# Macaron block on one core: the first step rebuilt, with four experts' weights spread by TensorE

## What is computed

```python
scores = sigmoid(x @ router_w.T); s = scores + bias        # 16 experts in 4 groups of 4
# best 2 groups by the sum of their two best s, then the best 4 experts in them
tw = scores[topk] / (sum + 1e-20) * 2.5                    # combine weights
h, u = einsum('td,edf->etf', x, gate_w), einsum('td,edf->etf', x, up_w)
y = einsum('etf,efd->etd', silu(h) * u, down_w)            # all 16 experts for all tokens
out = einsum('etd,te->td', y, combine) + shared_expert(x)  # shared: two more units of 128
```

## Time and profile before

| | us |
|---|---|
| median of 3 runs | 704.36 |
| profiled execution | 704.97 |
| its span on the core | 703.2 |
| TensorE busy | 667.4 (95%) |
| VectorE busy | 551.7 (78%) |
| GpSimd busy | 441.2 (63%) |
| ScalarE busy | 408.4 (58%) |

### The profile page before, as it was taken

How to read it: one execution, slowest core, us unless ns; L and a number is a source line. 1 busy time by engine, 2 the same in 40 slices (tenths; PEclk the granted TensorE clock), 3 DMA queues, 4 the chain that set the end, 5 groups by cost and what they waited for, 6 DMA issues and landing times.

```text
span 703.2 us, 11896 instructions
## 1 busy us (share of the span) xinstructions
PE 667.4 (95%) x3116; PEld 542.7 (77%) x3116; DVE 551.7 (78%) x1427; ACT 408.4 (58%) x812; POOL 441.2 (63%) x380
## 2 busy tenths in 40 slices
PE   4598999999999999999999999999999999999997
PEld 3386888888878878788776887768887888888885
DVE  4798887969697796977969869698697887969564
ACT  5465565565666545665456665566655565565553
POOL 4665666665766647665567565665657666666664
PEclk9699999999999999999999999999999999999999
DMA  8820633150605115042060320602406032240600
GB/s 230 264 93 4 239 121 121 33 209 2 240 1 195 47 31 212 0 152 89 6 236 0 123 118 17 240 0 100 156 15 240 11 147 100 70 188 17 240 15 16
DMA packets 30401, 76.31 MB, mean 109 GB/s; under 512 B 3584, under 2 KB 12304, under 8 KB 30352
## 3 DMA queue, kind: packets, MB, share of 16 engines
q1 hardware_dynamic: 30352, 75.79, 29.9%
HBM read 73.16 MB, written 2.62 MB: 108 GB/s over the span
## 4 chain that ended last, share of the span: by engine, by line
PE 64%; issue 12%; DVE 9%; POOL 9%; SPq 3%; DMA 1%; ACT 1%; DVEq 1%; POOLq 0%; ACTq 0%
POOL A_lo L319 8%; PE gateP L420 7%; PE gateP L422 7%; PE gateP L421 7%; PE upP L420 6%; PE upP L422 6%; PE upP L421 6%; PE yP L420 6%; PE yP L422 6%; PE yP L421 6%; DVE T L966 3%; SPq L255 1%; DVE A L988 1%; PE attP L466 1%; PE prepP L451 1%
## 5 line engine op out<-in xcount | busy, mean ns | idle before, releaser
L319 POOL TENSOR_TENSOR A_lo<-A,A_hi 128x512 fp32r<-128x512 f32 x288 | 370.9, 1292 | 193.5 <-ACT A_hi L708 193.3
L691 ACT ACTIVATE gateP<-gateP 128x512 f32<-128x512 f32 x256 | 148.7, 581 | 166.5 <-PE gateP L422 165.3
L966 DVE TENSOR_TENSOR T<-gateP,CB 128x512 f32<-128x512 f32 x256 | 175.1, 684 | 75.5 <-ACT gateP L691 67.8
L708 ACT CAST A_hi<-A 128x512 fp32r<-128x512 f32 x288 | 176.8, 614 | 74.9 <-DVE A L988 71.2
L988 DVE TENSOR_TENSOR A<-upP,T 128x512 f32<-128x512 f32 x256 | 176.9, 691 | 9.1
L420 PE MATMUL gateP<-XT_hi,W_hi 128*128 128x512 f32 x288 | 123.9, 430 | 13.9 <-DVE T L966 13.6
L420 PE MATMUL upP<-XT_hi,W_hi 128*128 128x512 f32 x288 | 114.7, 398 | 2.2 <-DVE A L988 2.2
L422 PE MATMUL gateP<-XT_lo,W_hi 128*128 128x512 f32 x288 | 113.8, 395 | 0.0
L420 PE MATMUL yP<-A_hi,W_hi 128*128 128x512 f32 x288 | 113.1, 393 | 0.6 <-POOL A_lo L319 0.6
L422 PE MATMUL upP<-XT_lo,W_hi 128*128 128x512 f32 x288 | 113.6, 395 | 0.0
L421 PE MATMUL gateP<-XT_hi,W_lo 128*128 128x512 f32 x288 | 113.5, 394 | 0.0
(11 more groups left out here) (162 smaller groups left out, 645.3 us busy)
## 6 DMA issues: line engine op xcount, KB each, us to landing
CB<-combT SPq DMA_DIRECT2D x128, 512.0 KB, 6.3
out_dram<-X SPq DMA_DIRECT2D x8, 256.0 KB, 2.0
X<-in_L_attn_x_dram SPq DMA_DIRECT2D x3, 512.0 KB, 6.0
W_in<-in_L_ffn_gate_w_dram SPq DMA_DIRECT2D x4, 256.0 KB, 4.8
W_in<-in_L_ffn_up_w_dram SPq DMA_DIRECT2D x4, 256.0 KB, 5.0
W_in<-in_L_ffn_down_w_dram SPq DMA_DIRECT2D x4, 256.0 KB, 5.2
X<-in_L_attn_x_dram SPq DMA_DIRECT2D x2, 256.0 KB, 4.3
combT<-CT SPq DMA_DIRECT2D x16, 32.0 KB, 1.8
```

The lines of the kernel that those rows point to most:

```text
L319: pool.tensor_tensor(A_lo[:, slot, :], A[:, slot, :], A_hi[:, slot, :].bitcast(F32), ALU.subtract).then_inc(low_done, 1)
L691: act.activation(dst, gateP[u % 2][:, :], ACT.Silu).then_inc(silu_done, 1)
L708: act.copy(A_hi[:, v % SLOTS, :], A[:, v % SLOTS, :]).then_inc(high_done, 1)
L966: dve.tensor_tensor(T[:, u % TS, :], gateP[u % 2][:, :], CB[:, e, :], ALU.mult).then_inc(gate_weighted, 1)
```

## The change

SP: the second half of X's first batch is loaded ahead of the shared weights instead of behind the first group of experts; of the other batches only batch 1 is loaded ahead of the first `CT` store, batches 2 and 3 and the small tensors behind the first step's `CB` loads. In step 0 the loads of experts 0 to 3 are left out.

TensorE: filler matmuls (`keep_busy`) at the start and ahead of the first `comb`; units 0 to 3 in an order of their own; experts 0 to 3 get their weights by `spread`, a transpose of a broadcast column of `comb`, into `backP` and `attP`; `transpose_weights(1)` moves from after unit 16 into unit 17; the setup transposes of the attention weights move from unit 6 to unit 20.

```diff
+    SPREAD = 4
+    WARM, FILL = 15, 10
 # SP
+            sp.dma_start(X[:, TILES:BT, :], x_v[0][:, TILES:BT, :]).then_inc(x_second, 16)
             ...
-                if g == 0:
-                    sp.dma_start(X[:, TILES:BT, :], ...).then_inc(x_second, 16)
-            for b in range(1, BATCH):
-                sp.dma_start(X[:, b * BT:(b + 1) * BT, :], x_v[b]).then_inc(x_rest, 16)
+            sp.dma_start(X[:, BT:2 * BT, :], x_v[1]).then_inc(x_third, 16)
             ...
-                for g in range(E // CSEM):
+                for g in range(SPREAD // CSEM if first else 0, E // CSEM):
             ...
             spread_weights(0, True)
+            for b in range(2, BATCH):
+                sp.dma_start(X[:, b * BT:(b + 1) * BT, :], x_v[b]).then_inc(x_rest, 16)
+            for dst, src in small:
+                sp.dma_start(dst, src).then_inc(small_in, 16)
 # GpSimd: constants first, then step_rstd(0), XA, and now
+            pool.wait_ge(xn_ready, 2)
+            step_rstd(1)
             ... # W_lo of units 2 and 3 in three pieces each, and in the pair
-                    if early and u < 3:
-                        split_low(2 * SHARED + 2 * u)
-                        split_low(2 * SHARED + 2 * u + 1)
-                    if early and w == 1:
-                        step_rstd(1)
+                    if early and u < AHEAD - 2 * SHARED:
+                        split_low(2 * SHARED + u)
 # TensorE
+            def spread(e):
+                for j in range(TILES):
+                    c = e * TILES + j
+                    mm = pe.transpose((backP, attP)[e % 2][:, j * P:(j + 1) * P],
+                                      comb[:, c:c + 1].broadcast_to([P, P]), ident[:, :])
+                mm.then_inc(spread_done, 1)
+            def keep_busy(count):
+                for _ in range(count):
+                    pe.matmul(yP[:, 0:P], ones[:, :], ones[:, :], start=True, stop=True)
+            def first_units():
+                for u in range(4):
+                    ... # waits: W_lo of u, XT_lo at u = 0, silu u - 2 from u = 2
+                    product(gateP[u % 2], ..gate..).then_inc(gate_done, 1)
+                    if u < 2:
+                        product(upP[u % 2], ..up..).then_inc(up_done, 1)
+                keep_busy(FILL)
+                pe.wait_ge(route_seq, ROUTE_OPS)
+                spread(0)
+                spread(1)
+                transpose_weights(0)
+                for u in (2, 3):
+                    pe.wait_ge(mul_done, u - 1)
+                    product(upP[u % 2], ..up..).then_inc(up_done, 1)
 # TensorE, pair: from unit 4
+                    if first and SHARED + 2 <= u < SHARED + SPREAD:
+                        pe.wait_ge(gate_weighted, u - SHARED - 1)
+                        spread(u - SHARED)
             ... # gate and up products of u
+                    if first and u == UNITS - 1:
+                        transpose_weights(1)
             ... # down product of u - 4
-                    if first and u == 6:
+                    if first and u == 20:
                         pe.wait_ge(small_in, 16 * 10)
-                        if w == (16 if early else 11):
+                        if w == 11 and not early:
                             transpose_weights(t0 + s + 1)
 # ahead of the pair
             pe.wait_ge(const_seq, IDENT_AT)
+            keep_busy(WARM)
 # ScalarE: W_hi of units 0, 1 ahead of XT; 2, 3 behind it; 4, 5 ahead of the pair;
 # 6 to 9 after silu 1; 10 and 11 in unit 3; 12 to 17 in units 4 to 9
+                        elif first and u < SHARED + SPREAD:
+                            if u >= SHARED + 2:
+                                act.wait_ge(mul_done, u - 1)
+                            dst = T[:, u % TS, :]
+                    if first and u in (3, 4):
+                        if u == 3:
+                            copy_weights(0)
+                        for v in (2 * u - 6, 2 * u - 5):
+                            round_high(n, v, False)
+                        if u == 3:
+                            split_high(AHEAD + 1)
 # VectorE
+                if isinstance(t, int) and t == 0 and e < SPREAD:
+                    dve.wait_ge(spread_done, e + 1)
+                    silu, weights = T[:, u % TS, :], (backP, attP)[e % 2][:, :]
             ...
-                    if early and w == 0:
-                        dve.wait_ge(x_second, 16)
-                        stats(1, 1)
-                    if first and u + AHEAD < UNITS:
-                        split_low(u + AHEAD)
+                    if first and 4 <= u and u - 4 + AHEAD < UNITS:
+                        split_low(u - 4 + AHEAD)
             ... # ahead of XT_lo
+            dve.wait_ge(x_second, 16)
+            rows(1, 1)
+            dve.wait_ge(rstd_ready, 2)
+            stats(1)
```

More of the change, by code:

```diff
@@ L236, in gate_left @@
         def gate_left(step, w):
-            if w < SHARED:
+            if w < SHARED or (isinstance(step, int) and step == 0 and w < SHARED + SPREAD):
                 return silu_done, UNITS * step + w + 1
@@ L311, in split_low @@
                 pool.wait_ge(w_hi_done, unit + 1)
-                pool.tensor_tensor(W_lo[:, unit, :, :], W_in[:, unit, :, :],
-                                   W_hi[:, unit, :, :].bitcast(F32),
-                                   ALU.subtract).then_inc(w_lo_done, 1)
+                if unit in (2, 3):
+                    for i in range(3):
+                        ins = pool.tensor_tensor(W_lo[:, unit, i, :], W_in[:, unit, i, :],
+                                                 W_hi[:, unit, i, :].bitcast(F32), ALU.subtract)
+                    ins.then_inc(w_lo_done, 1)
+                else:
+                    pool.tensor_tensor(W_lo[:, unit, :, :], W_in[:, unit, :, :],
+                                       W_hi[:, unit, :, :].bitcast(F32),
+                                       ALU.subtract).then_inc(w_lo_done, 1)
             def split_activations(n, slot):
@@ L520, in attention_stage @@
                         mm.then_inc(att_pe, 1)
+            def spread(e):
[9 more added lines that the diff above has]
+                for u in range(4):
+                    pe.wait_ge(w_lo_done, u + 1)
+                    if u == 0:
+                        pe.wait_ge(xt_lo_ready, 1)
+                    if u >= 2:
+                        pe.wait_ge(silu_done, u - 1)
+                    product(gateP[u % 2][:, :], W_hi[:, u, 0, :], W_lo[:, u, 0, :], XT_hi[:, 0, :],
+                            XT_lo[:, 0, :], True, True).then_inc(gate_done, 1)
+                    if u < 2:
+                        product(upP[u % 2][:, :], W_hi[:, u, 1, :], W_lo[:, u, 1, :], XT_hi[:, 0, :],
+                                XT_lo[:, 0, :], True, True).then_inc(up_done, 1)
+                keep_busy(FILL)
[5 more added lines that the diff above has]
+                    pe.wait_ge(mul_done, u - 1)
+                    product(upP[u % 2][:, :], W_hi[:, u, 1, :], W_lo[:, u, 1, :], XT_hi[:, 0, :],
+                            XT_lo[:, 0, :], True, True).then_inc(up_done, 1)
             def pair(p, first, attention, last, after=False):
                 n, t0 = PAIR * p, 2 * p
-                for u in range(PAIR + (LAG if last else 0)):
+                if first:
+                    first_units()
+                for u in range(4 if first else 0, PAIR + (LAG if last else 0)):
                     w, s = u % UNITS, u // UNITS
+                    if first and SHARED + 2 <= u < SHARED + SPREAD:
+                        pe.wait_ge(gate_weighted, u - SHARED - 1)
+                        spread(u - SHARED)
                     if u < PAIR:
@@ L674, in attention_stage, with round_high @@
                     act.copy(Bm[:, :], attP[:, 0:P]).then_inc(att_act, 1)
+            def round_high(n, v, filled):
+                act.wait_ge(mul_done, n + v + 1)
+                if filled:
+                    act.wait_ge(down_done, n + v + 1 - SLOTS)
+                act.copy(A_hi[:, v % SLOTS, :], A[:, v % SLOTS, :]).then_inc(high_done, 1)
             def pair(p, first, attention, last):
@@ L692, in pair @@
                     if first and u == 1:
-                        copy_weights(0)
-                    if first and u == 7:
+                        for unit in range(AHEAD - 4, AHEAD):
+                            split_high(unit)
+                    if first and u == 20:
                         act.wait_ge(setup_psum, 2)
@@ L699, in pair @@
                             act.copy(matrix[:, :], attP[:, i * P:(i + 1) * P]).then_inc(setup_sb, 1)
-                    if first and u + AHEAD < UNITS:
[L701 to L708, removed]
+                    if first and (u == 3 or 4 <= u and u - 2 + AHEAD < UNITS):
+                        split_high(AHEAD if u == 3 else u - 2 + AHEAD)
+                    if first and u in (3, 4):
[5 more added lines that the diff above has]
+                            split_high(AHEAD + 1)
```

(8 more changed lines are left out.)

62 lines of the change are left out of this document (32 added, 30 removed).

## The result

The changed kernel takes 698.75 us, median of 4 runs (697.64 to 698.80), against 704.14 us (702.83 to 705.14, 4 runs) before: ratio 0.9921, 95% interval 0.9901 to 0.9940. Run again beside three of the experiments it gave 699.07 (6 runs) and 0.9930 (0.9907 to 0.9953). The forecast was 698.1 (694.8 to 702.0). The profiled execution of the changed kernel is its fastest, 697.64 with a span of 695.9, that of before (704.97) lay above the median, so the two spans differ by 7.3 and the medians by 5.4. Executions over 1.5% above the fastest of the same kernel are left out of every comparison; there was one, the profiled execution of experiment 4, with 1880.42 us.

What follows compares the result with a forecast made beforehand. The prediction took VectorE to bound the first step once the load is gone, and TensorE the steady part. 6.7 us gained at unit 18 less 0.35 for setup transposes gave 6.3, hence 698.1 us by the medians, range 694.8 to 702.0.

Steps and rivals of the forecast that it cites:

- Once the load is gone, VectorE bounds the first step: First step without the wait for the CB load: VectorE, not TensorE, sets its time, 31.53 us with 29.60 busy before.
- unit 18: First unit of the second step: predicted to start at 60.55 against 67.24, 6.7 us gained.
- close behind: GpSimd in the first step: A_lo of unit 4 at 33.4, VectorE wanting unit 8's slot at about 34; hidden, by little.
- The load: Without the wait for the CB load, unit 2's multiply on VectorE starts at 21.45, 9.2 us before 30.68.
- my 4.4 us at 1.2 GHz: TensorE from 12.4: slow clock for 4.4 us, then the faster pitch, so FILL ends at 20.9 and opens the spreading.
- VectorE's account: VectorE from unit 2's multiply to unit 15's A: before 31.53 us, less 0.91 and 5.40, plus 8.6 for eight splits and 0.5.
- new waits: VectorE in the first step: one new wait, for ScalarE's silu 4, costing 0.5 us.
- a GpSimd queue without gaps: Case where each VectorE split waits for half of a 1.29 us A_lo: 1.2 rather than 1.08 each, sum 1 us worse.
- E: The end of unit 15's A on VectorE: 62.21 before, predicted 55.8, 6.4 us earlier.
- From E to unit 18: From unit 15's A to the second step: 4.75 us rather than 5.03, moving the comb transpose being worth 0.3.
- Loads: Late loads behind the first step's CB loads cost nothing; the first CB load, for unit 6, comes 0 to 0.6 late, taken as 0.
- the clock falls again after the spreading: Rival: TensorE at 1.2 GHz for two to three units after the spreading, 3.5 us lost, 701.6 us; chance 0.17.

Runs made afterwards that it cites:

- experiment 4: Changed kernel with AHEAD = 12, so GpSimd splits units 10 and 11 too and VectorE only six: 698.01 us, ratio 0.9917 to the kernel before.
- experiment 2: Changed kernel without VectorE's eight W_lo splits of step 0, those low parts set to zero once ahead of the routing: 694.19 us, ratio 0.9848.
- experiment 10: Changed kernel with the second operand of VectorE's eight W_lo splits read from PSUM instead of SBUF: 696.36 us, ratio 0.9885.
- experiment 1: Changed kernel without the spreading, experts 0 to 3 of step 0 taking their weights from the CB loads: 703.69 us, ratio 0.9993.
- experiment 3: Changed kernel without filler matmuls (WARM and FILL = 0): 698.95 us, ratio 0.9908.
- experiment 6: Changed kernel with X of batches 2 and 3 and the small tensors loaded ahead of the first CT store again: 698.62 us, ratio 0.9911.
- experiment 9: The control: the changed kernel run again unedited, beside three other runs, giving its second profile: 699.07 us, ratio 0.9930.
- experiment 7: Changed kernel with the transpose of step 1's combine weights back after unit 16: 699.08 us, ratio 0.9913.
- Experiment 11: Changed kernel with filler matmuls in TensorE's two waits of unit 17, three ahead of comb's transpose, four ahead of XN's: 699.82 us, ratio 0.9930.
- experiment 12: Changed kernel with AHEAD = 12, GpSimd splitting units 4 to 7 in thirds ahead of comb, and fillers in unit 17's waits: 698.04 us, ratio 0.9897.

## Why the prediction was right

**The bound.** "Once the load is gone, VectorE bounds the first step" is shown by experiments 2 and 10: taking VectorE's work or its stalls away, and nothing of TensorE's, brings 4.1 and 2.9 us at unit 18, and 4.6 and 2.7 by the medians. GpSimd's list, which I had called close behind, is unchanged in experiment 10, so it was not the bound either. The limit of it is new: without the splits VectorE waits for Silu, and by it mostly for TensorE, in units 5 to 8.

**The load.** I had put 9.2 between unit 2's two starts; it is 10.6. By experiment 1 the spreading itself is 5.7 of it and the other parts 4.9. I had called the spreading's start by FILL at 20.9 and by `comb` at 19.5. Measured: 19.39 and 18.99. The clock was at 2.4 GHz for XN's transposes and the logits, fell in the third matmul of the first product (11.90) and was back by 15.5, so FILL ended sooner than with my 4.4 us at 1.2 GHz. And `XT_lo`, which I let wait until 12.3, got in between GpSimd's two splits and was done at 11.2. Without WARM (experiment 3) it started 0.5 later, was held up and ended at 12.2, as I had it.

**VectorE's account.** Predicted 34.35 from unit 2 to E, measured 35.92. The splits were priced well, 8.6 against 8.82, and the new waits at 0.5 against 0.94: the wait for Silu in unit 4 is 0.38, and 0.56 is a wait that I had not seen, unit 2's `A` for TensorE's up product, which now stands behind the spreading. At a mean of 1.10 a split cost less than the 1.2 that I had worked out for a GpSimd queue without gaps. The term that I left out: `score` and `sel`, routing operations with two SBUF operands, met GpSimd and took 2.46 instead of 0.67 (0.45 and 0.22 before). I had seen `sel` at 0.92 in the earlier trace rows, priced it in the first routing and not in the second. Two other operations of the routing, `hi` and the first `ahead`, went the other way (0.50 and 0.39 before, 0.18 and 0.21 now). So E came at 56.01 for 55.8 because two misses of 1.4 and 1.6 cancel; the right time rests partly on that luck. In the second profile they are 1.8 and 1.3, and E is at 55.31.

**From E to unit 18.** Predicted 4.75, measured 4.75 (56.01 to 60.76), and 4.76 in experiment 1 (65.10 less 60.34): XN's transposes stand behind the CT copy, and the shorter wait before the transpose of `comb` (0.74 for 2.10) isn't a gain of that size: 4.75 against 5.03 before.

**Loads.** The store left at 20.86, CB's loads at 22.71, and unit 6 didn't wait; no cost, as said. That the late loads are no gain either, experiment 6 shows only by its time: their 1.3 us came back because `score` and `sel` happened to miss GpSimd.

**The rest.** I expected 636.3 behind unit 18 (0.35 of setup transposes added) and saw 635.1. From unit 20's multiply to the end the profiles have 628.5 (changed), 629.3 (before), 629.7 (control), 629.9 (experiment 3): executions differ by over 1 us there, for a reason that none of these runs looked for. By the medians the gain is 5.4 to 5.8, by unit 18 it is 6.5 to 7.2, and my 6.3 lies between the two; part of that gap may be the clock, below, though no run shows how much.

The rival "the clock falls again after the spreading" didn't happen in any profile with the spreading: the granted clock is 1.00 from 20 to 30. It was the right fear at the wrong place.

The Trainium skill, "SBUF — State Buffer", section "Who interferes with whom", says that a VectorE instruction with at most one SBUF input doesn't contend with GpSimd (outside the 2-port modes), while one with two SBUF inputs contends with a GpSimd instruction that reads SBUF. Experiment 10 agrees: a median of 0.54 against 1.28.

## What to carry to other kernels

When one wait is removed, write down the list of the engine that waited and add it up to the next point where the engines meet; that sum, not the length of the wait, gives the new time. In the sum, every two-operand VectorE operation on SBUF beside a busy GpSimd needs the price of the meeting, small ones too: here 0.2 us operations took 1.2. Fillers to hold TensorE's clock brought nothing measurable here, where another engine bounds what follows, and the clock mostly fell behind the short waits after them all the same.

## What the runs showed of the hardware that I had not expected

**The clock falls behind two short waits, in some executions.** TensorE waits about 0.75 and 1.15 us in unit 17, with one down product between them. Nine profiles of the changed kernel and its variants have these two waits, and in three of them (experiments 1, 2 and 3) the granted clock then went to 0.50. In experiment 7, with one wait of 2.10 instead, it fell too, while before the change it stayed at 1.00 behind the same 2.10. In experiment 3:

```profile
60.65 0.96 PE L456 MATMUL prepP<-ident,XN 128*128 128x128 f32 x4 [1.15 <-ACT CT L689]
```
```profile
60.00:64.00 4.00, 3.35 (x11) 0.60 0.05 12
```

From unit 18 to unit 20's multiply it takes 8.0 there (61.27 to 69.25) and 6.6 in the changed kernel, in the control and before: 1.4 us. The changed kernel and the control waited just as long and kept 1.00. What decides it, no run shows. The runs of one kernel spread over up to 5.3 us (experiment 6); how much of that is this fall, the runs don't tell either. Experiment 11 filled the waits, and its runs still spread over 2.2 us (the control's over 3.8).

**It falls behind WARM, too.** The fillers end between 6.9 and 8.2. Up to the first product TensorE then waits three times (0 to 1.5, 0.8 to 1.0 and 0.3 to 0.8 us), with XN's transposes and the logits between the waits. In nine of the eleven profiles with WARM the clock was at 0.50 by 12.3 and back by 15.5; in experiments 9 and 12 it stayed at 1.00 (the products' records are 0.39 long there instead of 0.63).

**A meeting costs both sides.** GpSimd's `A_lo`, 1.29 alone, took 1.60 in the changed kernel when a split of VectorE's got in first (25.89); with the operand in PSUM all of them took 1.27 to 1.32.
